# Expert stage: rstd for four tiles at once, scaling eight steps later; the expert weights applied by GpSimd and ScalarE

## The chip, the core and the metric

The kernel runs on one core of a Trainium2 chip. A core has TensorE (matrix products, results in PSUM), VectorE, ScalarE, GpSimd, and SyncE, which here only issues DMAs; each engine runs its own list of instructions in order, and semaphores tie them together. The time is the device time in microseconds (us) of one execution, as the median over several.

## What is computed

Two layers. Layer 0 (attention and feed-forward, eight sequences of 256 tokens, width 128) takes most of the time and isn't touched. The change is in the mixture of experts that ends layer 1, and in the sum that follows it:

```python
logits = xf @ router_w.T + router_b
top_w, top_e = jax.lax.top_k(softmax(logits), 2)          # 16 experts, 2 per token
top_w = top_w / jnp.sum(top_w, axis=-1, keepdims=True)
# for every expert, for the tokens routed to it:
h = jax.nn.silu(xf @ W1.T) * (xf @ W3.T)                  # 128 -> 256
y = h @ W2.T                                              # 256 -> 128
yn = (y - mean(y)) / jnp.sqrt(var(y) + 1e-05) * gm + bt
acc = acc + coeff[:, None] * yn
# and at last, s being layer 1's attention:
x = x + s * silu(acc)
```

## The kernel before

**Stages.** 2048 tokens are 16 tiles of 128 (NT = 16). A loop of four turns computes layer 0 and layer 1's attention; a last section computes routing, and GpSimd scatters every token's row to two places of a scratch tensor in HBM that is sorted by expert (L1854). Then comes the expert stage: CT = 48 tiles of 128 rows, each of one expert. It ends with a gather-free load of the results (they were sent to their tokens' places) and the output.

**The expert stage, tile by tile.** All engines run over steps j = 0 to 47 and a few more, each tile passing down the line:
- ScalarE copies the expert's weights W1, W3, gamma and beta into a ring of places (L1295, 128x768, PLACES = 12, two tiles ahead), applies Silu to the first half of the up product (L1308), and copies turned tokens for each pair of tiles (L1285).
- TensorE turns tokens (L1100), computes the up product (L1112, four 128x128 products a tile) and, two steps later, the down product (L1124, two products). All are recorded at the helper's line L782, the turns at L1100.
- VectorE in step j: statistics of tile j - 3 (bn_stats L1679), scale of tile j - 6 (L1686: YN times rstd plus beta, into the ring YO of eight), aggregate of tile j - 3 (L1692, mean and variance), product of tile j (L1697: Silu times the second half), centring of tile j - 3 (L1701: minus mean, times gamma, into the ring YN of four). SCALE_LAG = 6 is that distance of six.
- GpSimd for each pair of tiles: rstd (the helper at L1779 to L1782: variance plus EPS, then the power -0.5, both on 128x2), after both tiles' aggregates; then a send for each tile, two tiles behind (L1826: an indirect DMA that writes each row of YO to its token's place in HBM). Per pair the order is rstd(t, t+1), send(t-2), send(t-1). The scale of tile t waits for rstd(t, t+1) (c_rstd, L1681), the send of a tile for its scale (c_out), and the scale of tile s for the landing of the send of s - 8 (spread).

**After the last send.** SyncE waits until all sends have landed and loads the results in four groups of four token tiles, each 512 KB (L770, YAB: two results a token). For each group g VectorE multiplies both results by their router weights (L1718, two products of 128x512), adds them (L1722), ScalarE applies Silu (L1313), and VectorE multiplies by S1ALL and adds XALL (L1710, L1711), one group later. SyncE stores each group (L773). Every ScalarE activation is recorded at the helper's line L1132.

Of the kernel before, what the change touches and what calls it, by code (L numbers as in the profile page):

```python
# [18 lines left out]
ALU = mybir.AluOpType  # L19
# [3 lines left out]
P = 128  # L23
D = 128
NB, SEQ = 8, 256
NT = NB * SEQ // P
GT = 4
# [16 lines left out]
class Pair:  # L44
# [8 lines left out]
    def sem(self, n):  # L53
        return self.sems[n % 2]
# [366 lines left out]

DOWN_LAG, CENTRE_LAG, SCALE_LAG = 2, 3, 6

OUT_RING, MULT_RING, TOKEN_RING, NORM_RING = 8, 3, 8, 4

PLACES = 12
WIDE = 2 * FE + 2 * D

T_A0 = T_P_USES // 2
# [6 lines left out]
def gated_layers(nc, ins, out):  # L438
    ctx = ExitStack()
    with ctx:  # L440
# [3 lines left out]
        def sem(name):  # L444
            return ctx.enter_context(nc.semaphore(name))

        def pair(name):
            return Pair(ctx, nc, name)
# [55 lines left out]
        def carve(*shape):  # L504
            n = 1
            for s in shape:
                n *= s
            v = arena[:, at[0]:at[0] + n]
            at[0] += n
            assert at[0] <= ARENA, at[0]  # L510
            if len(shape) == 1:
                return v
            names = "abcd"[:len(shape)]
            return v.rearrange(f"p ({' '.join(names)}) -> p {' '.join(names)}",
                               **{c: s for c, s in zip(names[1:], shape[1:])})
# [105 lines left out]
        WUP = carve(PLACES, WIDE)  # L621
        YN = carve(NORM_RING, D)
        YO = carve(OUT_RING, D)
        YAB = carve(NT, 2, D)
        G2 = carve(2, GT, D)
        G3 = carve(2, GT, D)
# [21 lines left out]
        onehot, gap_done, gap_exp = sem("onehot"), sem("gap_done"), sem("gap_exp")  # L648
        pos_done, q_masked = sem("pos_done"), sem("q_masked")
        pv_done, iota_raw, iotas = pair("pv_done"), sem("iota_raw"), sem("iotas")  # L650
        moe_in, silu_done, out_ready = sem("moe_in"), sem("silu_done"), sem("out_ready")


# [9 lines left out]
        def down_bank(tile):  # L663
            return DOWN_BANKS[tile % len(DOWN_BANKS)][:, 0:D]
# [465 lines left out]
        def _(act):  # L1130
# [149 lines left out]
            def keep_pair(q):  # L1280
                act.wait_ge(c_turned, q + 1)
                t = 2 * q % TOKEN_RING
                if 2 * q >= TOKEN_RING:
                    act.wait_ge(c_up, 2 * q - TOKEN_RING + 2)
                act_fn(XGT[:, t:t + 2, :].rearrange("p j k -> p (j k)"), Tb[0][:, 0:2 * P], ACT.Copy).then_inc(c_ready, 1)  # L1285
# [16 lines left out]
            for j in range(CT):  # L1302
                if j + 2 < CT:
                    place_weights(j + 2)
                act.wait_ge(c_up, j + 1)
                if j >= 2:
                    act.wait_ge(c_mult, j - 1)
                act_fn(HS[:, j % 2, :], up_bank(j)[:, 0:FE], ACT.Silu).then_inc(c_silu, 1)  # L1308
                if j % 2 and j + 3 < CT:
                    keep_pair((j + 3) // 2)  # L1310
            for g in range(NT // GT):
                act.wait_ge(moe_in, g + 1)
                act_fn(G3[:, g % 2].rearrange("p t d -> p (t d)"), G2[:, g % 2].rearrange("p t d -> p (t d)"), ACT.Silu)\  # L1313
                    .then_inc(silu_done, 1)
# [3 lines left out]
        def _(dve):  # L1318
# [9 lines left out]
            def step(instr, carry_wait=True):  # L1328

                steps[1] += 1  # L1330
                instr.then_inc(dstep, 1)
                dve.wait_ge(dstep, steps[0] + steps[1])
                if not carry_wait:
                    settled()
# [337 lines left out]
            for j in range(CT + SCALE_LAG):  # L1672
                tile, scaled = j - CENTRE_LAG, j - SCALE_LAG
                centres = 0 <= tile < CT
                n, w = tile % NORM_RING, WUP[:, tile % PLACES, 2 * FE:WIDE]
                if centres:
                    dve.wait_ge(c_down, tile + 1)
                    settled()
                    V.bn_stats(ST[:, n, 0, :], down_bank(tile)).then_inc(c_bn, 1)  # L1679
                if scaled >= 0:  # L1680
                    dve.wait_ge(c_rstd, scaled // 2 + 1)  # L1681
                    dve.wait_ge(c_centred, scaled + 1)
                    if scaled >= OUT_RING:

                        dve.wait_ge(spread[scaled % OUT_RING], 16 * (scaled // OUT_RING))
                    V.scalar_tensor_tensor(YO[:, scaled % OUT_RING, :], YN[:, scaled % NORM_RING, :],  # L1686
                                           RS[:, scaled % NORM_RING:scaled % NORM_RING + 1],
                                           WUP[:, scaled % PLACES, 2 * FE + D:WIDE], ALU.mult, ALU.add).then_inc(c_out, 1)
                if centres:
                    dve.wait_ge(c_bn, tile + 1)  # L1690
                    settled()
                    V.bn_aggr(MV[:, n, :], ST[:, n, 0, :]).then_inc(c_stats, 1)  # L1692
                if j < CT:
                    dve.wait_ge(c_silu, j + 1)
                    if j >= MULT_RING:
                        dve.wait_ge(c_down, j - MULT_RING + 1)
                    V.tensor_tensor(GTT[:, j % MULT_RING, :], HS[:, j % 2, :], up_bank(j)[:, FE:2 * FE], ALU.mult)\  # L1697
                        .then_inc(c_mult, 1)
                if centres:
                    dve.wait_ge(c_stats, tile + 1)  # L1700
                    V.scalar_tensor_tensor(YN[:, n, :], down_bank(tile), MV[:, n, 0:1], w[:, 0:D], ALU.subtract, ALU.mult)\  # L1701
                        .then_inc(c_centred, 1)
            steps[:] = [c0, 0]

# [7 lines left out]

            for g in range(NT // GT):
                x = slice(g * GT, (g + 1) * GT)
                dve.wait_ge(ld_y[g], 16)
                for k in range(2):
                    y = YAB[:, x, k, :]
                    last = V.tensor_tensor(y, y, WGT[:, k, x].unsqueeze(2).broadcast_to([P, GT, D]), ALU.mult)  # L1718
                step(last)
                if g >= 2:  # L1720
                    dve.wait_ge(silu_done, g - 1)
                V.tensor_tensor(G2[:, g % 2], YAB[:, x, 0, :], YAB[:, x, 1, :], ALU.add).then_inc(moe_in, 1)  # L1722
                if g:
                    output(g - 1)
# [4 lines left out]
        def _(pool):  # L1729
# [49 lines left out]
            def rstd(o, var):  # L1779
                n = var.shape[1]  # L1780
                step(G.tensor_scalar(o, var, EPS, None, ALU.add))  # L1781
                return G.tensor_tensor(o, o, powm[:, 0:n], ALU.pow)  # L1782
# [75 lines left out]

            steps[:] = [step_c0, 0]
            for tile in range(CT):  # L1860
                if tile % 2 == 0:
                    pool.wait_ge(c_stats, tile + 2)
                    if tile >= 4:
                        pool.wait_ge(c_out, tile - 2)
                    rstd(RS[:, tile % 4:tile % 4 + 2], MV[:, tile % 4:tile % 4 + 2, 1]).then_inc(c_rstd, 1)
                if tile >= 2:
                    send(tile - 2)
            send(CT - 2)
            send(CT - 1)


def rope_tables():
# [39 lines left out]
```

## Time and profile before

| | us |
|---|---|
| median of three runs | 936.89 (935.74 to 938.36) |
| profiled execution | 931.56 |
| its span, first to last instruction | 929.7 |

| engine | busy us | share of the span |
|---|---|---|
| TensorE (PE) | 727.6 | 78% |
| VectorE (DVE) | 635.4 | 68% |
| ScalarE (ACT) | 506.0 | 54% |
| GpSimd (POOL) | 391.5 | 42% |

Engines appear in the profile as PE, PEld (TensorE's weight load), DVE, ACT, POOL and SP (SyncE). The table of shares is a mean over stages with different limits. The expert stage starts where the tokens' rows come back from HBM, at about 806 us, and its last send is issued at 907.78; the rest is the final sum. A row of the timeline gives start, duration, engine, line, operation, output and inputs, how often it was repeated, and in square brackets the idle time before it with what ended that. An operation's idle time of kind "issue" is the engine's own sequencing.

### The profile page before, as it was taken

The page shows a single profiled execution, that of the slowest core. Times are in us where ns is not written, and L with a number is a line of the kernel's source. Part 1 is how long each engine was busy: PE and PEld are TensorE (multiplying, and loading weights), DVE is VectorE, ACT ScalarE, POOL GpSimd, SP SyncE. Part 2 cuts the span into 40 slices and gives each one's busy share as a digit, 9 for nine tenths or more (in the row PEclk, how much of TensorE's full clock was granted, in tenths as well). Part 3 has the DMA queues.
Part 4 walks back from the last instruction along what each step waited for, and adds up shares of the span by engine and source line. Part 5 has one row for each costly group of instructions (what it writes and reads, how often), then busy time and mean ns, then how long its engine had stood idle before and what let it go on. Part 6 is the DMA issues. An engine that isn't in the chain of part 4 may idle for free.

```text
span 929.7 us, 19949 instructions
## 1 busy us (share of the span) xinstructions
PE 727.6 (78%) x6997; PEld 547.7 (59%) x7031; DVE 635.4 (68%) x1521; ACT 506.0 (54%) x901; POOL 391.5 (42%) x470
## 2 busy tenths in 40 slices
PE   2589787599898875898988769885997689698840
PEld 1256465367676753576767447762775567598730
DVE  2586685588779664977796759638676499276645
ACT  1255455365766653756766446543656275487711
POOL 4560651670335034705340545009300437458880
PEclk9799998799999997999999979989999599899975
DMA  5700000000000000000000000000000345212104
GB/s 154 213 1 1 1 1 1 1 1 2 1 2 1 2 1 2 1 2 1 2 1 2 1 2 1 2 1 0 2 2 1 92 135 180 84 59 80 59 38 144
DMA packets 41963, 29.70 MB, mean 32 GB/s; under 512 B 7570, under 2 KB 39308, under 8 KB 41612
## 3 DMA queue, kind: packets, MB, share of 16 engines
q1 hardware_dynamic: 39308, 23.18, 8.6%
q0 software_dynamic: 2560, 5.25, 1.5%
q8 instruction: 60, 0.98, 0.4%
q14 instruction: 35, 0.29, 0.1%
HBM read 18.98 MB, written 9.44 MB: 31 GB/s over the span
## 4 chain that ended last, share of the span: by engine, by line
PE 44%; DVE 20%; POOL 12%; issue 12%; ACT 8%; DMA 1%; SPq 1%; DVEq 0%; POOLq 0%; ACTq 0%
PE psM L782 19%; PE psT L821 4%; ACT arena L1132 4%; PE psO L866 4%; PE psS L851 4%; DVE arena L1457 3%; PE psO L782 3%; PE psS L812 3%; DVE PR L1349 3%; POOL arena L1800 3%; POOL arena L1803 3%; POOL yt_scratch L1826 3%; ACT L1132 2%; POOL RS L1782 2%; DVE arena L1465 2%
## 5 line engine op out<-in xcount | busy, mean ns | idle before, releaser
L782 PE MATMUL psM<-arena 128*128 128x128 f32 (+7 forms) x1168 | 269.3, 374 | 48.0 <-DVE arena L1457 30.3
L1132 ACT ACTIVATE arena<-psT 128x512 f32<-128x512 f32 (+3 forms) x296 | 149.6, 530 | 128.6 <-PE psT L821 44.9
L782 PEld LDWEIGHTS psM<-arena 128*128 128x128 f32 (+5 forms) x1168 | 158.6, 193 | 102.0 <-DVE arena L1457 44.3
L1132 ACT ACTIVATE arena<-psM 128x512 f32<-128x512 f32 (+2 forms) x168 | 88.4, 542 | 126.6 <-PE psM L782 125.7
L1781 POOL TENSOR_SCALAR RS<-MV 128x2 f32<-128x2 f32 x56 | 12.9, 231 | 304.0 <-DVE MV L1490 211.6
L1343 DVE TENSOR_REDUCE MX<-psS 128x4 f32<-128x512 f32 (+1 forms) x160 | 102.7, 683 | 44.9 <-PE psS L851 22.9
L1800 POOL TENSOR_TENSOR arena<-arena,powm 128x8 f32<-128x8 f32 x64 | 109.5, 1711 | 5.3
L1132 ACT ACTIVATE PR<-PR 128x512 f32<-128x512 f32 x160 | 94.9, 626 | 21.0 <-DVE PR L1349 20.7
L1349 DVE TENSOR_TENSOR PR<-psS,MX 128x512 f32<-128x512 f32 x160 | 102.2, 680 | 0.0
L821 PE MATMUL psT<-ident,PR 128*128 128x128 f32 x640 | 91.4, 278 | 10.5 <-ACT PR L1132 6.8
L821 PEld LDWEIGHTS psT<-ident,PR 128*128 128x128 f32 x640 | 71.9, 143 | 34.3 <-issue 22.9
L1803 POOL TENSOR_TENSOR arena<-arena 128x512 f32<-128x512 f32 x64 | 84.1, 1313 | 0.0
L1457 DVE TENSOR_TENSOR arena<-psM,arena 128x512 f32<-128x512 f32 x128 | 81.8, 681 | 3.3 <-POOL arena L1803 3.3
L1132 ACT ACTIVATE arena<-arena 128x768 f32 (+3 forms) x61 | 46.5, 763 | 57.1 <-DVE arena L1722 30.2
L1132 ACT ACT_TABLE_LOAD x51 | 65.4, 1283 | 2.1 <-PEq L1904 1.2
L1799 POOL TENSOR_SCALAR arena<-arena 128x8 f32<-128x8 f32 x64 | 18.2, 284 | 109.9 <-DVE arena L1448 109.3
L1465 DVE TENSOR_TENSOR arena<-arena 128x512 f32<-128x512 f32 x64 | 49.9, 802 | 19.8 <-POOL arena L1803 19.8
L782 PEld LDWEIGHTS psO<-arena,PT 128*64 128x64 f32 (+1 forms) x768 | 48.2, 155 | 14.9 <-issue 11.3
L1448 DVE TENSOR_REDUCE arena<-arena 128x8 f32<-128x512 f32 x64 | 43.5, 679 | 19.5 <-ACT arena L1132 19.1
L851 PE MATMUL psS<-arena 32*128 32x256 f32 (+1 forms) x512 | 55.7, 346 | 0.0
L1826 POOL DMA_INDIRECT yt_scratch<-arena,DEST x48 | 49.9, 1040 | 12.2 <-issue 6.7
L782 PE MATMUL psO<-arena,PT 128*64 128x65 f32 (+1 forms) x768 | 51.5, 241 | 2.9 <-ACT PT L1132 2.9
(196 smaller groups left out, 1142.5 us busy)
## 6 DMA issues: line engine op xcount, KB each, us to landing
arena<-in_L_ffn_w SPq DMA_DIRECT2D x50, 128.0 KB, 2.4
xg_scratch<-zeros SPq DMA_DIRECT2D x12, 256.0 KB, 4.0
arena<-xg_scratch SPq DMA_DIRECT2D x12, 256.0 KB
arena<-yt_scratch SPq DMA_DIRECT2D x4, 512.0 KB, 5.3
arena<-in_L_ffn_wqkv SPq DMA_DIRECT2D x2, 768.0 KB, 5.0
arena<-in_L_ffn_ln_g SPq DMA_DIRECT2D x1, 1024.0 KB, 7.5
arena<-in_L_ffn_ln_b SPq DMA_DIRECT2D x1, 1024.0 KB, 10.4
out<-arena SPq DMA_DIRECT2D x4, 256.0 KB, 2.2
```

The costliest lines, as they stand in the source:

```text
L782: return nc.tensor.matmul(o, lhsT, rhs, start=start, stop=stop)
L821: last = nc.tensor.transpose(bank[:, c * P:(c + 1) * P], PR[:, m % 4, c * P:(c + 1) * P], ident[:])
L851: last = nc.tensor.matmul(Sb[i][:, c * keys:(c + 1) * keys], QL[r, b, lane, qt * P:(qt + 1) * P], KT1[r, b * SEQ:b * SEQ + keys], start=False,
L1132: return nc.scalar.activation(o, i, f, **kw)
L1343: V.tensor_reduce(maxima[i], scores[i], AX, ALU.max).then_inc(dstep, 1)
L1349: V.tensor_tensor(PR[:, (n + i) % 4, :].rearrange("p (s k) -> p s k", s=ns), scores[i], maxima[i].unsqueeze(2).broadcast_to([P, ns, 512 // ...
L1448: V.tensor_reduce(SS[:, m % 4, :], SQ[:, m % 2, :].rearrange("p (h d) -> p h d", h=8), AX, ALU.add).then_inc(ss_done.sem(m), 1)
L1457: last = V.tensor_tensor(dst.rearrange("p (h d) -> p h d", h=8), src, RT[:, 2 * l + n % 2, x, t % 2, :].unsqueeze(1) .broadcast_to([P, 8, ...
L1465: V.tensor_tensor(r1, r1, RN[:, m % 4, :].unsqueeze(2).broadcast_to([P, 8, DH]), ALU.mult)\
L1800: G.tensor_tensor(RN[:, m % 4, :], RN[:, m % 4, :], powm[:, 0:8], ALU.pow)
L1803: G.tensor_tensor(r1, r1, r2[:, :, ::-1, :], ALU.add).then_inc(rope_sum.sem(m), 1)
L1826: G.indirect_dma_start(YT, bass.IndirectOffsetOnAxis(DEST[:, tile:tile + 1], 0), YO[:, tile % OUT_RING, :], None)\
```

## The change

- SCALE_LAG goes from 6 to 8, the rings of statistics and of YN (NORM_RING) from 4 to 8, the places for weights from 12 to 14. The expert stage gets its own tiles for statistics, mean and variance, and rstd, in the arena.
- GpSimd computes rstd for four tiles at once (TOGETHER = 4), and sends one tile behind instead of two. Per four tiles the order is rstd(t to t+3), send(t-1), send(t), send(t+1), send(t+2).
- The weighting leaves VectorE. GpSimd multiplies the first result of each group (one product 128x512), after its last send; ScalarE multiplies the second (four Copies 128x128 with a scale per partition), one group ahead of its Silu. VectorE waits for both and adds.

```diff
-DOWN_LAG, CENTRE_LAG, SCALE_LAG = 2, 3, 6
-OUT_RING, MULT_RING, TOKEN_RING, NORM_RING = 8, 3, 8, 4
-PLACES = 12
+DOWN_LAG, CENTRE_LAG, SCALE_LAG = 2, 3, 8
+OUT_RING, MULT_RING, TOKEN_RING, NORM_RING = 8, 3, 8, 8
+PLACES = 14
+TOGETHER = 4
...
+        C_STATS, C_MEAN, C_RSTD = carve(NORM_RING, 6), carve(NORM_RING, 2), carve(NORM_RING)
...
+            def weight_second(g):
+                act.wait_ge(ld_y[g], 16)
+                for t in range(g * GT, (g + 1) * GT):
+                    last = act_fn(YAB[:, t, 1, :], YAB[:, t, 1, :], ACT.Copy, scale=WGT[:, 1, t:t + 1])
+                last.then_inc(second_weighted, 1)
+
+            weight_second(0)
             for g in range(NT // GT):
+                if g + 1 < NT // GT:
+                    weight_second(g + 1)
                 act.wait_ge(moe_in, g + 1)
...
-                    V.bn_stats(ST[:, n, 0, :], down_bank(tile)).then_inc(c_bn, 1)
+                    V.bn_stats(C_STATS[:, n, :], down_bank(tile)).then_inc(c_bn, 1)
                 if scaled >= 0:
-                    dve.wait_ge(c_rstd, scaled // 2 + 1)
+                    dve.wait_ge(c_rstd, scaled // TOGETHER + 1)
...
-                                           RS[:, scaled % NORM_RING:scaled % NORM_RING + 1],
+                                           C_RSTD[:, scaled % NORM_RING:scaled % NORM_RING + 1],
...
-                dve.wait_ge(ld_y[g], 16)
-                for k in range(2):
-                    y = YAB[:, x, k, :]
-                    last = V.tensor_tensor(y, y, WGT[:, k, x].unsqueeze(2).broadcast_to([P, GT, D]), ALU.mult)
-                step(last)
+                dve.wait_ge(first_weighted, g + 1)
+                dve.wait_ge(second_weighted, g + 1)
                 if g >= 2:
                     dve.wait_ge(silu_done, g - 1)
                 V.tensor_tensor(G2[:, g % 2], YAB[:, x, 0, :], YAB[:, x, 1, :], ALU.add).then_inc(moe_in, 1)
...
             for tile in range(CT):
-                if tile % 2 == 0:
-                    pool.wait_ge(c_stats, tile + 2)
-                    if tile >= 4:
-                        pool.wait_ge(c_out, tile - 2)
-                    rstd(RS[:, tile % 4:tile % 4 + 2], MV[:, tile % 4:tile % 4 + 2, 1]).then_inc(c_rstd, 1)
-                if tile >= 2:
-                    send(tile - 2)
-            send(CT - 2)
+                if tile % TOGETHER == 0:
+                    pool.wait_ge(c_stats, tile + TOGETHER)
+                    if tile >= NORM_RING:
+
+                        pool.wait_ge(c_out, tile - NORM_RING + TOGETHER)
+                    x = slice(tile % NORM_RING, tile % NORM_RING + TOGETHER)
+                    rstd(C_RSTD[:, x], C_MEAN[:, x, 1]).then_inc(c_rstd, 1)
+                if tile:
+                    send(tile - 1)
             send(CT - 1)
+            for g in range(NT // GT):
+                x = slice(g * GT, (g + 1) * GT)
+                pool.wait_ge(ld_y[g], 16)
+                G.tensor_tensor(YAB[:, x, 0, :], YAB[:, x, 0, :], WGT[:, 0, x].unsqueeze(2).broadcast_to([P, GT, D]),
+                                ALU.mult).then_inc(first_weighted, 1)
```

## Rows read from the trace of the kernel before

**Rows 1.** Table of stretches: us; busy per engine (instructions); clock; DMA share; GB/s

```profile
838.00:897.00 59.00, 48.60 (x396) 45.24 (x394) 38.17 (x163) 37.41 (x73) 49.17 (x65) 1.00 0.17 59
```

**Rows 2.** Timeline of GpSimd, one pair of tiles in mid stage

```profile
847.64 0.24 POOL L1781 TENSOR_SCALAR RS<-MV 128x2 f32<-128x2 f32 x1
847.96 0.72 POOL L1782 TENSOR_TENSOR RS<-RS,powm 128x2 f32<-128x2 f32 x1
848.88 1.13 POOL L1826 DMA_INDIRECT yt_scratch<-arena,DEST  x1 [0.20 <-issue]
850.31 0.96 POOL L1826 DMA_INDIRECT yt_scratch<-arena,DEST  x1 [0.30 <-DVE arena L1686]
851.30 0.24 POOL L1781 TENSOR_SCALAR RS<-MV 128x2 f32<-128x2 f32 x1
```

**Rows 3.** Timeline, VectorE's two scales of the same pair

```profile
848.72 0.35 DVE L1686 SCALAR_TENSOR_TENSOR arena<-arena,RS 128x128 f32<-128x128 f32 x1 [1.31 <-POOL RS L1782]
...
849.85 0.33 DVE L1686 SCALAR_TENSOR_TENSOR arena<-arena,RS 128x128 f32<-128x128 f32 x1
```

**Rows 4.** Timeline of TensorE, down products of two tiles two apart

```profile
823.06 0.61 PE L782 MATMUL psT<-arena 128*128 x4
...
825.96 0.61 PE L782 MATMUL psO<-arena 128*128 x4
```

**Rows 5.** Groups by line and shape: count, busy us, mean ns, idle before: the power

```profile
L1800 POOL TENSOR_TENSOR arena<-arena,powm 128x8 f32<-128x8 f32 x64 | 109.5, 1711 | 5.3
...
L1782 POOL TENSOR_TENSOR RS<-RS,powm 128x2 f32<-128x2 f32 x56 | 40.5, 723 | 4.7
```

**Rows 6.** Timeline of GpSimd: second rstd, first and last send

```profile
821.90 0.23 POOL L1781 TENSOR_SCALAR RS<-MV 128x2 f32<-128x2 f32 x1 [1.65 <-DVE MV L1692]
...
823.11 1.07 POOL L1826 DMA_INDIRECT yt_scratch<-arena,DEST  x1 [0.18 <-issue]
...
907.78 0.96 POOL L1826 DMA_INDIRECT yt_scratch<-arena,DEST  x1 [0.30 <-issue]
```

**Rows 7.** Timeline of VectorE: the scales in steps 8, 9 and 10

```profile
824.39 0.33 DVE L1686 SCALAR_TENSOR_TENSOR arena<-arena,RS 128x128 f32<-128x128 f32 x1
...
825.85 0.33 DVE L1686 SCALAR_TENSOR_TENSOR arena<-arena,RS 128x128 f32<-128x128 f32 x1
...
827.33 0.34 DVE L1686 SCALAR_TENSOR_TENSOR arena<-arena,RS 128x128 f32<-128x128 f32 x1
```

**Rows 8.** Timeline of VectorE after the last send: its first and its last operation

```profile
913.88 1.29 DVE L1718 TENSOR_TENSOR arena<-arena,WGT 128x512 f32<-128x512 f32 x2 [9.61 <-DMA arena<-yt_scratch]
...
926.31 0.69 DVE L1711 TENSOR_TENSOR arena<-arena,XALL 128x512 f32<-128x512 f32 x1
```

**Rows 9.** Timeline in layer 0, both engines reading SBUF: VectorE from 208.09, GpSimd

```profile
208.09 2.37 DVE L1465 TENSOR_TENSOR arena<-arena 128x512 f32<-128x512 f32 x2
...
208.30 1.61 POOL L1803 TENSOR_TENSOR arena<-arena 128x512 f32<-128x512 f32 x1
```

**Rows 10.** Timeline in the routing: a GpSimd send and VectorE's operation beside it

```profile
777.98 1.89 POOL L1854 DMA_INDIRECT xg_scratch<-XN1ALL,POSU  x1 [0.30 <-issue]
...
777.82 1.22 DVE L1659 TENSOR_TENSOR arena<-arena 128x1024 bf16<-128x1024 f32 x1
```

**Rows 11.** View of single lines: count, ns min/median/max, first and last start, shape

```profile
L1803 POOL TENSOR_TENSOR arena<-arena x64: 1253/1272/1702, 23.6 to 653.7; 128x512 f32<-128x512 f32 x64
...
L1814 POOL TENSOR_SCALAR arena<-arena,lanem x32: 917/922/1032, 190.6 to 745.2; 128x256 f32<-128x256 f32 x32
```

**Rows 12.** Groups by shape, ScalarE, without and with scale and bias per partition

```profile
L1132 ACT ACTIVATE arena<-psM 128x256 f32<-128x256 f32 x40 | 14.2, 375 | 34.6 <-PE psM L782 34.6
L1132 ACT ACTIVATE arena<-psT,arena 128x256 f32<-128x256 f32 x16 | 9.0, 561 | 18.2 <-PE psT L985 18.2
```

**Rows 13.** View of the results' scratch tensor: its four loads

```profile
L770 SPq DMA_DIRECT2D arena<-yt_scratch x4: 359/934/1447, 910.1 to 912.4; - x4
...
DMA to landing us min/median/max: 3.8/5.3/5.9
```

More of the change, by code:

```diff
@@ L650, in gated_layers @@
         pv_done, iota_raw, iotas = pair("pv_done"), sem("iota_raw"), sem("iotas")
+        first_weighted, second_weighted = sem("first_weighted"), sem("second_weighted")
         moe_in, silu_done, out_ready = sem("moe_in"), sem("silu_done"), sem("out_ready")
@@ L1691, in _ @@
                     settled()
-                    V.bn_aggr(MV[:, n, :], ST[:, n, 0, :]).then_inc(c_stats, 1)
+                    V.bn_aggr(C_MEAN[:, n, :], C_STATS[:, n, :]).then_inc(c_stats, 1)
                 if j < CT:
@@ L1700, in _ @@
                     dve.wait_ge(c_stats, tile + 1)
-                    V.scalar_tensor_tensor(YN[:, n, :], down_bank(tile), MV[:, n, 0:1], w[:, 0:D], ALU.subtract, ALU.mult)\
+                    V.scalar_tensor_tensor(YN[:, n, :], down_bank(tile), C_MEAN[:, n, 0:1], w[:, 0:D], ALU.subtract, ALU.mult)\
                         .then_inc(c_centred, 1)
```

## The prediction

> **What bounds the kernel now.** I read the table of stretches first, because the change touches only the expert stage and what follows it. In the middle of that stage, 838 to 897 us, no compute engine is full: TensorE 48.6 of 59 us, VectorE 38.2, ScalarE 37.4, GpSimd 49.2 [rows 1]. But the profile counts an issuing interval of GpSimd as idle, so its timeline has to be read next. One pair of tiles there is add EPS 0.24, a gap of 0.08, power 0.72, 0.20 of issue, a send of 1.13, 0.30 of issue, a send of 0.96, and 0.03 later the next add: 3.66 us, with no place in it where GpSimd waits for anybody [rows 2]. VectorE's timeline says the same from the other side: in each pair its first scale (L1686) has stood idle for 1.31 us, released by GpSimd's power, and the second scale starts 1.13 after the first [rows 3]. Without that wait VectorE needs 3.66 - 1.31 = 2.35 us a pair. TensorE, while it was the limit, needed 2.90 (823.06 to 825.96) [rows 4]. So the expert stage runs at GpSimd's 3.66, and a faster GpSimd gains until 2.90. TensorE's granted clock is 1.00, its 2.4 GHz level, through this stretch [rows 1] and stays out of the sum. After the last send (907.78) the kernel is a chain: send landed, load of the gathered results, then VectorE back to back from 913.88 to 927.0, then the last store [rows 6, 8].
>
> **Deviations of four tiles at once.** Twelve groups of four replace 24 pairs. The only unknown is the power on 128x4. On 128x2 it takes 723 ns, on 128x8 1711 [rows 5]; a straight line gives 1.05; the mean of the wide ones holds some that were disturbed, so I take 1.04. Bounds: 0.72 (width free below four) and 1.44 (twice the pair). The add, 0.24 now, I take at 0.25 [rows 2]. A cycle of four tiles becomes: send 1.13, three times (0.30 + 0.96), 0.03, add 0.25, 0.08, power 1.04, 0.20 of issue = 6.51 us, against 2 x 3.66 = 7.32. TensorE's floor for four tiles is 5.80, so GpSimd stays the bound, by 0.70.
>
> **Scaling eight steps later.** The first deviation now needs four tiles of statistics. They are there at 821.8 (the second pair's add starts at 821.90 [rows 6]), so the wide one ends about 823.3. The send of tile 0 no longer follows the scale of step 6 but that of step 8, which started at 824.39 [rows 7]: with its 0.33 and some 0.3 of waking and issue it starts at 825.0, not 823.11 [rows 6]. Sends of tiles 1 and 2 follow the scales of steps 9 and 10 (825.85, 827.33 [rows 7]), so at 826.5 and 827.97; the second wide deviation runs 829.0 to 830.34, and the send of tile 3 starts at 830.54. From there GpSimd is continuous: ten cycles of 6.51 to the send of tile 43 (895.64), 1.43 and three times 1.26 to that of tile 47: 900.85. Before it was 907.78 [rows 6]. The stage gives **6.9 us**. (Had the late start cost nothing, 11 cycles would have given 8.9.)
>
> Does the new wait hold GpSimd? The deviation of four needs the statistics of step t+6, the scale reads it in step t+8. When it ends, VectorE, which waits in step t+8, is released; GpSimd issues four sends, 5.1 us, before it wants the statistics of step t+10. VectorE needs under three steps for that, 3 x 1.13 from its own work (4.4 at TensorE's pace). Slack 0.7 or more. Sends sit one tile closer to their scales than before; each needs the scale of a tile whose step is 1.13 after the last, against 1.26 between sends, so none waits. ScalarE's copies of weights wait for the scale of a tile further back; with the places raised from 12 to 14 that distance is as it was. The eight-deep ring YO: the scale of tile s needs the send of s-8 landed, issued 5 us or more before. All at nothing; if the first slack were gone, every us past it costs 11 us in all.
>
> **A port between VectorE and GpSimd.** The trace shows the two holding each other up. At 208.09 two VectorE adds with both inputs in SBUF take 2.37 together (two such operations undisturbed: 1.29 [rows 8]), around a GpSimd add that itself takes 1.61 instead of some 1.27 [rows 9]: GpSimd waited for the running add, and then the next VectorE add waited for the whole of GpSimd's. A send is held too: 1.89 instead of 0.96, under a VectorE tensor_tensor of 1.22 begun just before [rows 10]. So the 1.13 of the first send after a deviation is 0.96 plus what is left of the scale (it runs from 848.72 to 849.07, the send starts at 848.88 [rows 2, 3]). I keep that 0.17 once in four tiles; the other three start some 0.1 to 0.3 after a scale has ended.
> The Trainium skill (SBUF — State Buffer, Who interferes with whom) infers that a tensor_tensor leaves descriptor generation alone, since that needs only the write interface. By it no send would ever pay for a scale: the sum would stay as it is, and rival (d) and half of (b) below would fall away. Rows 10 say otherwise for these indirect sends, and I go by the rows.
>
> **Weighting moved off VectorE.** Removed: eight VectorE products, 1.29 for two [rows 8], some 1.23 with the overlap of 0.07 into the next; 4 x 1.23 = 4.9 us of a chain that is solid VectorE. Added: GpSimd, four products 128x512; the add of that size has 1.27 as its median, 1.25 as its least [rows 11], and I take 1.26, since it too reads two tensors. The bound above is the product with a scalar per partition, 0.92 for half the size, so 1.8 [rows 11]; ScalarE, 16 Copies of 128x128 with a scale per partition. Its rows: 128x256 from PSUM is 0.38, with a scale and a bias per partition 0.56 [rows 12], so 0.09 for one; 128x128 then some 0.4, overlapping by 0.1, four of them 1.3. The loads of y land 3.8 to 5.9 us after issue, the first at 913.88, the last near 918.3, 1.5 apart [rows 13].
> Without the port: first sum can start at 915.37 (913.95 + 1.26, ScalarE 1.3), the second after its landing, 916.8; ScalarE does the second group's weighting before its first Silu, so output 0 starts 917.6; then VectorE is solid: 4 outputs of 1.3 and 2 sums of 0.65, end 924.1. That would be 2.9 less than 927.0.
> With the port: every remaining VectorE operation reads two SBUF tensors, and so does GpSimd's. Sum 0 runs 915.37 to 916.05 and holds product 1 back to 917.3. GpSimd's product 2 follows at once, sum 1 waits behind it to 918.53 and ends 919.2, holding product 3, which gets in before output 0 and runs to 920.4. Left are then four outputs of 1.25 and two sums of 0.63: 926.7. Gain **0.3 us**. (With products of 1.8, the same steps end at 928.9, 1.9 later than now.) The forecast takes this case, as rows 9 show just this alternation with these two kinds of operation.
> The same page of the Trainium skill states it as a rule: a VectorE instruction with two SBUF inputs and a GpSimd instruction that reads SBUF exclude each other for the whole instruction. By that rule the tail gives 0.3, by no rule 2.9; the trace agrees with the rule.
>
> **Sum.** Profiled execution 931.56 (span 929.7): minus 6.9, minus 0.3, 924.4. The median of the three runs is 936.89; the profiled one lies 5.3 under it, and I assume the gap is the same for both kernels: 936.89 - 7.2 = **929.7**.
>
> **Rivals.** (a) *The tail is free of the port*: stage 6.9, tail 2.9, 927.1. For it: product 3 and the two Silus may interleave more kindly than I drew. Against it: rows 9. With the narrow power as well (0.72, 11 x 0.32 = 3.5) it is 923.6.
> (b) *Power grows with width, or sends meet scales*: at 1.44 the cycle is 6.91, 11 x 0.40 = 4.4 is lost, which makes 934.1. The same happens if each of the other three sends pays 0.17: 0.51 x 11 = 5.6, 935.3. For it: VectorE is released in bursts, and later steps of a burst may be set by TensorE. Against: the line between two widths, and the distances above.
> (c) *The late start eats what the cycle gives, no change*: a cycle of 7.1 or more, 936 to 939. It needs both halves of (b), or one with products of 1.8.
> (d) *Slower*: the sends fall into step with the scales. VectorE's scale of 0.34 reads two SBUF tensors; if in the cycle each of three sends starts with a scale just begun, each pays 0.34, the cycle is 6.51 + 1.02 = 7.53, and 11 x 1.02 = 11.2 is lost: 929.7 + 11.2 = 940.9. It decides against the change from 0.22 us a send (7.2 / 33). Against it: the second send of each pair does not pay now [rows 2].
> (e) *The change doesn't do what it says*: the power is issued for four tiles, but VectorE, not GpSimd, turns out to set the pace. VectorE's 2 x 2.35 = 4.7 per four tiles excludes it.
>
> **How the numbers follow.** The forecast with its small variations 0.60; (a) 0.14; (b) 0.17; (c) 0.05; (d) 0.04. I leave (c), (d) and the far end of (a) outside, reach to 925.3 (half of the narrow power with the free tail) and to 934.4 (inside b). About 0.3% (2.8 us) is what a measurement of this kernel tells from no change, so faster ends at 934.1: the forecast, (a) and about two thirds of (b), 0.86; same 0.09, slower 0.05.
>
> **What would show each step.** Timeline of GpSimd in mid stage: a power on 128x4 of 1.04 and 6.51 us from one to the next; first send near 825.0 and last near 900.9; the scale still waits for the power, about 1.8 us once in four tiles (6.51 less 4.7). If instead GpSimd idles before the add, the new wait binds and the forecast is wrong. If sends two to four of a cycle read more than 0.96, it is (b) or (d). In the tail: GpSimd products of 1.7 and VectorE sums of 1.8 mean the port; 1.27 and 0.69 mean (a); 1.8 for the very first product, which nothing disturbs, means the dear product.

## The result and the profile after

| | before | changed |
|---|---|---|
| median of 14 runs each, us | 934.45 | 928.75 |
| span of the profiled execution, us | 929.7 | 924.1 |

The ratio is 0.9937, with a 95% interval from 0.9918 to 0.9956: 0.63% or about 5.9 us faster (the medians differ by 5.7), where 7.2 were forecast against the first three runs.

To see where the time went I cut both profiled executions at the same events: VectorE's first product in the expert stage, the last send, the first operation on loaded results, VectorE's last end, and the end of the span.

| stretch, us | before | changed | difference | forecast |
|---|---|---|---|---|
| start to first product (nothing changed here) | 814.53 | 815.37 | +0.84 | 0 |
| first product to last send | 93.25 | 87.01 | -6.24 | -6.9 |
| last send to first operation on its results | 6.10 | 6.33 | +0.23 | 0 |
| from there to VectorE's last end | 13.12 | 12.65 | -0.47 | -0.3 |
| to the end of the span | 2.70 | 2.74 | +0.04 | 0 |

The first line is scatter, not the change: over all kernels shown below, whose work up to there is the same, it lies between 813.4 and 818.3. The spans of single profiles should therefore be compared by stretches.

The timeline of GpSimd in the changed kernel, mid stage, one cycle of four tiles; it answers to [rows 2]:

```profile
849.74 0.25 POOL L1791 TENSOR_SCALAR arena<-arena 128x4 f32<-128x4 f32 x1
850.08 1.04 POOL L1792 TENSOR_TENSOR arena<-arena,powm 128x4 f32<-128x4 f32 x1
851.32 1.15 POOL L1836 DMA_INDIRECT yt_scratch<-arena,DEST  x1 [0.20 <-issue]
852.77 0.96 POOL L1836 DMA_INDIRECT yt_scratch<-arena,DEST  x1 [0.30 <-DVE arena L1699]
854.04 0.96 POOL L1836 DMA_INDIRECT yt_scratch<-arena,DEST  x1 [0.30 <-DVE arena L1699]
855.30 0.96 POOL L1836 DMA_INDIRECT yt_scratch<-arena,DEST  x1 [0.30 <-issue]
856.28 0.25 POOL L1791 TENSOR_SCALAR arena<-arena 128x4 f32<-128x4 f32 x1
```

From add to add it is 6.54 us, still without a wait: the gap ahead of a send is the 0.30 of issue whatever the profile names as its releaser, and ahead of the add it is 0.02. The power on 128x4 takes 1.04. From the same timeline the first and the last send, which answer to [rows 6], and between them VectorE's scale that waits for the power, which answers to [rows 3]:

```profile
826.11 1.09 POOL L1836 DMA_INDIRECT yt_scratch<-arena,DEST  x1 [1.66 <-DVE arena L1699]
...
851.15 0.35 DVE L1699 SCALAR_TENSOR_TENSOR arena<-arena 128x128 f32<-128x128 f32 x1 [1.91 <-POOL arena L1792]
...
902.38 0.96 POOL L1836 DMA_INDIRECT yt_scratch<-arena,DEST  x1 [0.30 <-issue]
```

The end of the kernel, which answers to [rows 8]: the timeline of all engines from the first loaded group on.

```profile
908.71 1.28 ACT L1136 ACTIVATE arena<-arena,WGT 128x128 f32<-128x128 f32 x4 [21.55 <-DMA arena<-yt_scratch]
908.76 1.03 POOL L1884 TENSOR_TENSOR arena<-arena,WGT 128x512 f32<-128x512 f32 x1 [5.42 <-DMA arena<-yt_scratch]
910.09 0.69 DVE L1732 TENSOR_TENSOR arena<-arena 128x512 f32<-128x512 f32 x1 [11.99 <-ACT arena L1136]
...
912.37 1.12 POOL L1884 TENSOR_TENSOR arena<-arena,WGT 128x512 f32<-128x512 f32 x1 [0.69 <-DMA arena<-yt_scratch]
912.50 1.53 DVE L1723 TENSOR_TENSOR arena<-arena,S1ALL 128x512 f32<-128x512 f32 x1
...
914.07 0.69 DVE L1724 TENSOR_TENSOR arena<-arena,XALL 128x512 f32<-128x512 f32 x1
914.10 1.55 POOL L1884 TENSOR_TENSOR arena<-arena,WGT 128x512 f32<-128x512 f32 x1 [0.62 <-DMA arena<-yt_scratch]
914.68 1.53 DVE L1732 TENSOR_TENSOR arena<-arena 128x512 f32<-128x512 f32 x1
...
919.95 0.69 DVE L1723 TENSOR_TENSOR arena<-arena,S1ALL 128x512 f32<-128x512 f32 x1 [0.48 <-DMA out<-arena]
```

Here is the port. VectorE's output at 912.50 stands behind GpSimd's product that began at 912.37 and ends at 913.49: 1.53 instead of 0.68. GpSimd's last product begins at 914.10 under a running VectorE operation and takes 1.55 instead of 1.03; the sum at 914.68 then waits for it, 1.53 again. These are the only two operations of VectorE in the tail that the port stretches. Two things in these rows were not in the forecast: the groups land 1.8 us apart, and the last output (919.95) waits 0.48 for a store to leave its buffer.

### The profile page after: what moved, and what is told of

Same layout as the page of the kernel before. It is cut to its first block, busy times and chain, and to the rows that moved or that the text cites. A ratio compares the mean times of both kernels' runs of the same rounds, so it can differ in the third digit from the quotient of the medians.

```text
span 924.1 us, 19925 instructions
## 1 busy us (share of the span) xinstructions
PE 724.8 (78%) x6997; PEld 546.0 (59%) x7031; DVE 632.7 (68%) x1513; ACT 510.2 (55%) x917; POOL 387.6 (42%) x450
## 4 chain that ended last, share of the span: by engine, by line
PE 45%; DVE 19%; issue 12%; POOL 12%; ACT 8%; DMA 2%; SPq 1%; DVEq 0%; ACTq 0%; POOLq 0%
PE psM L786 19%; PE psT L825 5%; ACT arena L1136 5%; PE psO L870 4%; PE psS L855 4%; DVE arena L1470 3%; PE psO L786 3%; PE psS L816 3%; POOL yt_scratch L1836 3%; DVE PR L1362 3%; POOL arena L1813 3%; POOL arena L1810 3%; ACT L1136 2%; DVE arena L1461 1%; DVE arena L1478 1%
## 5 line engine op out<-in xcount | busy, mean ns | idle before, releaser
L1791 POOL TENSOR_SCALAR RS<-MV 128x2 f32<-128x2 f32 x32 | 7.2, 224 | 286.4 <-DVE MV L1503 211.8
```

## The experiments

e3, e4, e5, e6, e10 and e11 were executed once each; of these only the stretches and rows of their profiles are used.

**Which half of the change gives the gain.** Stage alone (VectorE weights as before), and tail alone (the stage as before):

```diff
-                dve.wait_ge(first_weighted, g + 1)
-                dve.wait_ge(second_weighted, g + 1)
+                dve.wait_ge(ld_y[g], 16)
+                for k in range(2):
+                    y = YAB[:, x, k, :]
+                    last = V.tensor_tensor(y, y, WGT[:, k, x].unsqueeze(2).broadcast_to([P, GT, D]), ALU.mult)
+                step(last)
```

That is e1_stage_alone against the changed kernel (weight_second and GpSimd's products go too). e2_tail_alone is the kernel before with the same lines the other way round, and with weight_second and the products added.

> Only the expert stage is changed (deviations of four, scales eight steps later); VectorE weights both results as before. Read as two stretches: from VectorE's first product to the last send (before 93.25 us, after 87.01), and from the first VectorE operation after the last send to VectorE's last end (before 13.12). Theory, the stage carries nearly all: 87.0 and 13.1, ratio to the kernel before about 0.994. Rival, the moved weighting carries a good part of the gain: then this kernel stands at 0.996 or above.

> Only the weighting is moved; the stage is as before. Theory, the port between VectorE and GpSimd gives back most of what is taken off VectorE: stage 93.3, from the landing of the first results to VectorE's last end 12.7 instead of 13.1, ratio 0.9995, no measurable difference. Rival, the port costs little: 10.5 and a ratio of 0.997.

| | first product to last send | to first operation | to VectorE's last end | ratio to before (95%) |
|---|---|---|---|---|
| before | 93.25 | 6.10 | 13.12 | |
| changed | 87.01 | 6.33 | 12.65 | 0.9937 (0.9918 to 0.9956) |
| e1_stage_alone | 86.38 | 6.40 | 13.12 | 0.9945 (0.9918 to 0.9972) |
| e2_tail_alone | 92.74 | 6.12 | 12.24 | 0.9997 (0.9978 to 1.0017) |

The stage carries the gain: its stretch is as short in e1 as in the changed kernel, and without it (e2) nothing is left in the runs. The interval of e1 alone would allow the 0.996 of the rival too. The moved weighting by itself can't be told from no change, though its stretch is 0.9 us shorter in the profile. It is 12.24 there and 12.65 in the changed kernel, with the same instructions; that is followed up below. The stage's 0.6 of difference between two kernels with the same stage is how far the start of the stage scatters (first send 10.03 after the first product in one, 10.74 in the other).

**What the later scale costs.** The changed kernel with deviations of two tiles:

```diff
-TOGETHER = 4
+TOGETHER = 2
```

> The changed kernel with deviations of two tiles again, everything else kept: scales eight steps later, rings of eight. The later scale alone. Theory: the first send comes 10.6 after the first product (before 8.6), GpSimd has one pair's deviation more behind it, 23 cycles of 3.66 follow as before: from the first product to the last send 96.0, 2.8 more than in the kernel before. Rival: the later scale costs nothing, 93.3.

First send 10.76 after the first product, last send 96.36: 3.1 us later than before. The first send accounts for 2.2 of it; the other 0.9 is about one pair's deviation, which stood ahead of the first send and now stands behind it, as e5 also keeps the new order of the sends. The whole run took 938.32 beside 930.31 for the kernel before on the same chip, but those are one run each, and the kernel before alone ranges over 9 us. Moving the scale is a pure cost, and the groups of four pay for it.

**What GpSimd's adds and powers hide.** The changed kernel without them:

```diff
-                    dve.wait_ge(c_rstd, scaled // TOGETHER + 1)
+                    dve.wait_ge(c_stats, scaled + 1)
...
-                                           C_RSTD[:, scaled % NORM_RING:scaled % NORM_RING + 1],
+                                           C_MEAN[:, scaled % NORM_RING, 1:2],
...
-                if tile % TOGETHER == 0:
-                    pool.wait_ge(c_stats, tile + TOGETHER)
...
-                    rstd(C_RSTD[:, x], C_MEAN[:, x, 1]).then_inc(c_rstd, 1)
                 if tile:
                     send(tile - 1)
```

> The changed kernel without any add and power on GpSimd in the expert stage: VectorE scales by the variance itself, the deviation is left out. GpSimd has only sends, 1.26 a tile. Theory, TensorE is the next bound at 2.90 a pair: from the first product to the last send 74 to 76 us instead of 87.0. Rival, VectorE or ScalarE sets 1.6 a tile: 80. Of the sends: if the 1.13 of a cycle's first send is a wait for the scale running beside it, sends above 0.96 stay wherever a scale has begun just before; if it is the price of the first send after another GpSimd operation, none is left but the first.

77.42 us instead of 87.01, a little over the 74 to 76, with the first send at 11.45 after the first product instead of 10.7 (why it is later wasn't followed up). The table of stretches of this kernel (columns as in [rows 1]):

```profile
838.00:885.00 47.00, 46.90 (x421) 46.71 (x419) 40.31 (x165) 38.65 (x79) 30.91 (x33) 1.00 0.25 82
```

Its timeline, two sends a pair apart and two of TensorE's down products a pair apart:

```profile
854.34 0.95 POOL L1836 DMA_INDIRECT yt_scratch<-arena,DEST  x1 [0.39 <-DVE arena L1699]
...
855.30 0.61 PE L786 MATMUL psO<-arena 128*128 x4
...
857.24 0.95 POOL L1836 DMA_INDIRECT yt_scratch<-arena,DEST  x1 [0.36 <-DVE arena L1699]
...
858.19 0.61 PE L786 MATMUL psO<-arena 128*128 x4
```

TensorE is busy 46.90 of 47 us and both engines step by 2.9 us a pair: the floor that the prediction took from [rows 4]. GpSimd now waits for VectorE ahead of sends. On the sends' own price this run says half: without powers none of the 48 reads over 0.96, but none of them starts inside the stretch of a scale that costs (below), so it doesn't speak of the port.

**Where the 1.13 of a cycle's first send comes from.** The prediction gave it to the port. First a memset, then a power, ahead of the fourth send of a cycle:

```diff
+                if tile % TOGETHER == 3:
+                    G.memset(POOL_SPARE[:], 0.0)
                 if tile:
                     send(tile - 1)
```

In e11_power_before_send the new line is `G.tensor_tensor(POOL_SPARE[:], WGT[:, 0, 0:2], powm[:, 0:2], ALU.pow)`.

> The changed kernel with a GpSimd memset of 128x2 before the fourth send of every cycle of four. If the first send's 1.13 is a wait for VectorE's scale, the fourth send stays at 0.96 and the cycle grows by the memset alone. If a send costs more after any other GpSimd operation, the fourth send reads about 1.13 too and the cycle grows by that besides.

> The changed kernel with one more power of 128x2 (its result isn't used) ahead of the fourth send of each cycle of four; a memset there left that send at 0.96. If the send after a power costs more by itself, the fourth reads about 1.07 though no scale runs beside it; if the 1.15 of the first send is all a wait for the scale, the fourth stays at 0.96. The cycle grows from 6.55 to about 7.2 either way, as in the rival (a price of the power by its count), and the last send comes 7 us later.

The timeline of e6, a second send with VectorE's scale beside it, and a fourth send behind its memset:

```profile
833.35 0.33 DVE L1700 SCALAR_TENSOR_TENSOR arena<-arena 128x128 f32<-128x128 f32 x1
...
833.44 1.09 POOL L1837 DMA_INDIRECT yt_scratch<-arena,DEST  x1 [0.30 <-issue]
...
848.89 0.12 POOL L1880 MEMSET POOL_SPARE<- 128x2 f32 x1
849.20 0.97 POOL L1837 DMA_INDIRECT yt_scratch<-arena,DEST  x1 [0.19 <-issue]
```

The timeline of e11, a fourth send behind its power, with VectorE's last scale before it and the next one after it:

```profile
848.14 0.33 DVE L1700 SCALAR_TENSOR_TENSOR arena<-arena 128x128 f32<-128x128 f32 x1
...
848.60 0.73 POOL L1880 TENSOR_TENSOR POOL_SPARE<-WGT,powm 128x2 f32<-128x2 f32 x1
849.52 1.03 POOL L1837 DMA_INDIRECT yt_scratch<-arena,DEST  x1 [0.19 <-issue]
...
852.00 0.35 DVE L1700 SCALAR_TENSOR_TENSOR arena<-arena 128x128 f32<-128x128 f32 x1 [2.63 <-POOL arena L1793]
```

A send after a memset costs what the others cost, and the memset's 0.12 fits into the gap of issue (the cycle stays 6.54 to 6.57). A send after a power costs 1.03 though the scale at 848.14 had ended a microsecond before: 0.07 go with the power. And a second send, with no power ahead of it, reads 1.09 where a scale had begun 0.09 before it (833.44): the port is real too, as in [rows 10]. The power itself shows its price: the cycle grows from 6.55 to 7.27 and the last send comes at 95.44, 8.4 us later, where 7 were expected.

How the 1.15 splits is read from other sends. The changed kernel's very first send (826.11, shown further up) stands behind a power of 128x4. Its timeline, the scale before that send, and a second send of a cycle with the scale before it:

```profile
825.48 0.34 DVE L1699 SCALAR_TENSOR_TENSOR arena<-arena 128x128 f32<-128x128 f32 x1
...
832.93 0.33 DVE L1699 SCALAR_TENSOR_TENSOR arena<-arena 128x128 f32<-128x128 f32 x1
...
833.06 1.03 POOL L1836 DMA_INDIRECT yt_scratch<-arena,DEST  x1 [0.30 <-issue]
```

The same of e4, its very first send, with no power ahead of it:

```profile
828.75 0.96 POOL L1836 DMA_INDIRECT yt_scratch<-arena,DEST  x1 [22.27 <-DVE arena L1699]
```

The first send, at 826.11, starts 0.29 after its scale has ended and still reads 1.09; without powers it reads 0.96. So 0.13 goes with the power of 128x4, although that had ended 1.66 us earlier. The send at 833.06 meets the last 0.20 of a scale and reads 0.07 more than 0.96; the first send of a cycle meets the last 0.18. The 1.15 is therefore nearer to 0.96 + 0.13 + 0.06, and the scale has the smaller part. Why the power of 128x2 in e11 left only 0.07 is open. In all kernels here, sends behind another send read 1.01 to 1.09 where a scale had begun 0.09 to 0.17 before them (12 sends), and 0.95 to 0.97 where it had begun 0.19 or more before; sends that started within 0.02 of a scale's start read 0.96.

**What the port costs in the tail.** Without GpSimd's products, and with them only for the groups where VectorE is idle anyway:

```diff
-                V.tensor_tensor(G2[:, g % 2], YAB[:, x, 0, :], YAB[:, x, 1, :], ALU.add).then_inc(moe_in, 1)
+                if g < 2:
+                    V.tensor_tensor(G2[:, g % 2], YAB[:, x, 0, :], YAB[:, x, 1, :], ALU.add).then_inc(moe_in, 1)
+                else:
+                    for t in range(g * GT, (g + 1) * GT):
+                        last = V.scalar_tensor_tensor(G2[:, g % 2, t % GT, :], YAB[:, t, 0, :], WGT[:, 0, t:t + 1],
+                                                      YAB[:, t, 1, :], ALU.mult, ALU.add)
+                    last.then_inc(moe_in, 1)
```

That is e7_products_two_groups, whose GpSimd loops over two groups and whose VectorE waits for it in those two only. In e3_no_gpsimd_product the loop on GpSimd and VectorE's wait for it are gone, and the sum is as in the changed kernel.

> The changed kernel without GpSimd's four products: the first result of each token goes into the sum unweighted, that part of the computation is left out. ScalarE's part, the loads and VectorE's work are the same. Theory, the port: VectorE's sums and outputs all at 0.69, and from the first landing to VectorE's last end 10.2 instead of 12.65. Rival, the loads that land 1.8 apart and ScalarE's weighting ahead of its Silu set the tail: 12 or more.

> The changed kernel, with GpSimd's product only for groups 0 and 1, where VectorE has idle time anyway; for groups 2 and 3 VectorE multiplies and adds in one pass (four scalar_tensor_tensor of 128x128 a group, some 1.15 us, instead of a sum of 0.69). If the port is what makes the tail long, from the first landing to VectorE's last end it is 11.1 instead of 12.65 (after), although VectorE has more work; if VectorE's work or the loads set it, 13.0 or more.

The stretch from the first landing to VectorE's last end is 12.65 in the changed kernel, 10.90 without the products, 11.36 with two of them. So the products beside VectorE cost 1.75 us, and the two stretched operations, 1.53 instead of 0.68 and 0.69, are 1.69 of it: that is the port. Giving VectorE more work (1.13 for a multiply and add of four tiles, against 0.69 for the sum) makes the tail 1.3 us shorter, since nothing then stands in its way (11.1 were expected for the 11.36; the intervals of the whole runs of e7 and of the changed kernel overlap, so this too rests on the profile). The 10.90 is over the 10.2 expected: 0.49 of it is the wait for a store's buffer, and the second group lands 1.8 after the first. VectorE's timeline without the products:

```profile
910.30 0.69 DVE L1731 TENSOR_TENSOR arena<-arena 128x512 f32<-128x512 f32 x1 [11.92 <-ACT arena L1136]
912.10 0.69 DVE L1731 TENSOR_TENSOR arena<-arena 128x512 f32<-128x512 f32 x1 [1.11 <-ACT arena L1136]
912.71 0.68 DVE L1723 TENSOR_TENSOR arena<-arena,S1ALL 128x512 f32<-128x512 f32 x1
...
918.47 0.69 DVE L1723 TENSOR_TENSOR arena<-arena,S1ALL 128x512 f32<-128x512 f32 x1 [0.49 <-DMA out<-arena]
```

**Why the loads land later.** In the kernel before and in e2_tail_alone the four loads move about 347 GB/s and land up to 5.9 us after issue [rows 13]; in the changed kernel and in every other one up to here it is about 290 GB/s and up to 7.0 or 7.1. e1_stage_alone has the tail of before and is slow, e2_tail_alone has the new tail and is fast, so it isn't what the engines do meanwhile; what goes with it is the layout. The new tiles for statistics (48 + 16 + 8 numbers) push YAB from a multiple of 512 bytes in the arena to 288 past one. (The arena itself starts at byte 65024 of a partition, 127 times 512; in e6 and e11 POOL_SPARE moves it 32 bytes on, which puts YAB at 320 past a multiple.)

```diff
+        carve(56)
         YAB = carve(NT, 2, D)
```

That is e9_results_at_512; e10_results_at_64 has 8 in place of 56.

> The changed kernel with 56 unused numbers (224 bytes) a partition ahead of the tile for the results (YAB). The change put 72 new numbers there, so YAB begins 288 bytes past a multiple of 512 (before: at a multiple of 512, counted in the arena), and in every run with the new layout its loads move 290 GB/s instead of 347. Theory, the start address: with the padding the loads are back at 347 GB/s and land 3.8 to 5.9 after issue instead of 4.0 to 7.0; from the last send to the first operation 6.1 instead of 6.33, from there to VectorE's last end 12.2 instead of 12.65: 0.6 to 0.7 us in all. Rival, what slows the loads is ScalarE and GpSimd working beside them, or chance: 290 GB/s as now.

> As e9_results_at_512 with only 8 numbers (32 bytes) of padding: YAB begins at 320 past a multiple of 512, at a multiple of 64. If it is a boundary of 64 bytes that matters, the loads move 347 GB/s; if one of 512, they stay at 290 or between.

Two microseconds in the middle of the loads, from the table of stretches (the last column is GB/s), first in the kernel before:

```profile
914.40:916.40 2.00, 0.00 (x0) 0.00 (x0) 1.97 (x4) 0.47 (x1) 0.00 (x0) 0.50 1.15 347
```

The same in the changed kernel, and from the view of its load line the landings, which answer to [rows 13]:

```profile
909.20:911.20 2.00, 0.00 (x0) 0.00 (x0) 0.69 (x1) 1.47 (x6) 1.23 (x2) 0.50 1.16 291
```

```profile
DMA to landing us min/median/max: 4.0/6.0/7.0
```

In e9:

```profile
908.10:910.10 2.00, 0.00 (x0) 0.00 (x0) 0.69 (x1) 1.78 (x7) 1.54 (x2) 0.50 1.15 347
```

```profile
DMA to landing us min/median/max: 3.8/5.4/5.9
```

In e10:

```profile
907.40:909.40 2.00, 0.00 (x0) 0.00 (x0) 0.69 (x1) 1.46 (x6) 1.23 (x2) 0.50 1.17 290
```

```profile
DMA to landing us min/median/max: 4.1/6.1/7.0
```

With YAB back at a multiple of 512 the loads are at 347 GB/s, beside the same work of ScalarE and GpSimd. From the last send to the first operation it is 6.16, the tail 12.23: 0.6 us less in all, as expected. At 320 past a multiple of 512, which is a multiple of 64, nothing changes. The whole kernel came to 0.9918 (0.9888 to 0.9947) of before; its interval overlaps that of the changed kernel, so the 0.6 us rests on the profile.

The Trainium skill (DMA: Bandwidth & Descriptors, How a descriptor splits into AXI transactions) says that a transaction of at most 256 bytes starts at a multiple of 256, so that a descriptor that doesn't start at one also pays for the bytes before it. Each packet here is 512 bytes; by that account (an estimate) it takes three transactions instead of two at both 288 and 320, and both are slow, so the runs agree with the page in that. The page also counts beats of 32 bytes, by which such packets would cost 6% and 12% more (an estimate), while both measure the same, 290 for 347 GB/s. Nor do the runs show 256 itself: none put YAB at an odd multiple of it, and the page's account is of a descriptor's reads, while here the misplaced end is the one written.

**Putting the findings together.** e7 with the first four tiles in two pairs and their scales six steps later (e8), and that with the padding of e9 as well (e12). GpSimd's loop follows GROUPS too; that part isn't shown:

```diff
 TOGETHER = 4
+GROUPS = [(0, 2), (2, 2)] + [(t, 4) for t in range(4, CT, 4)]
+STEP_OF = {s: s + (6 if s < 4 else 8) for s in range(CT)}
...
-                tile, scaled = j - CENTRE_LAG, j - SCALE_LAG
+                tile = j - CENTRE_LAG
+                scaled = next((s for s in STEP_OF if STEP_OF[s] == j), -1)
```

> As e7_products_two_groups, and the first four tiles go in two pairs with scales six steps later; from tile 4 on groups of four and eight steps. If the late start costs what the prediction put on it, the first send comes 8.6 us after the first product instead of 10.7, the cycle stays 6.55, and the last send comes 1.5 us earlier than in the changed kernel: 85.5 instead of 87.0. Rival: the ring and TensorE's pace take it up later, 87.0. Ratio to the kernel before 0.991 against 0.9925.

> The early start, GpSimd's product for groups 0 and 1 only, and the padding, together. From the first product to the last send 85.4, to the first operation after it 6.1, from there 10.9: against the changed kernel 1.6 + 0.2 + 1.7 = 3.5 us less, 9.4 less than the kernel before, ratio 0.990. If the parts overlap, 2 us less than the changed kernel and 0.992.

| | first send | last send | to first operation | to VectorE's last end | median, us | ratio to before (95%) |
|---|---|---|---|---|---|---|
| changed | 10.74 | 87.01 | 6.33 | 12.65 | 928.75 | 0.9937 (0.9918 to 0.9956) |
| e7_products_two_groups | 10.74 | 87.00 | 6.39 | 11.36 | 925.62 | 0.9919 (0.9888 to 0.9950) |
| e8_early_start | 7.07 | 85.44 | 6.41 | 11.35 | 925.92 | 0.9918 (0.9887 to 0.9948) |
| e12_best | 7.06 | 85.52 | 6.07 | 11.23 | 923.96 | 0.9900 (0.9874 to 0.9925) |

(The two sends are counted from the first product.) The early start gives its 1.5 us in the stretch, though between e7 and e8 the runs show no difference. Its first send came at 7.07 where 8.6 were expected, because it now stands ahead of the second pair's deviation; of these 3.7 us against the changed kernel 1.6 are left at the last send, as GpSimd then waits for VectorE, 0.93 us ahead of its third add and 0.37 and 0.71 ahead of two sends. So the rival of e8, that the pace of the others takes it up, is right for the larger half. From GpSimd's timeline of e8:

```profile
829.92 0.23 POOL L1801 TENSOR_SCALAR arena<-arena 128x4 f32<-128x4 f32 x1 [0.93 <-DVE arena L1708]
...
834.60 0.96 POOL L1846 DMA_INDIRECT yt_scratch<-arena,DEST  x1 [0.71 <-DVE arena L1702]
```

e12 is 3.2 us below the changed kernel over the three stretches, 1.49 + 0.26 + 1.42, where 3.5 were expected (its tail is 11.23 and not 10.9), and 1% below the kernel before. Its interval overlaps the end of that of the changed kernel, so as a whole the step from one to the other is likely and not settled.

## Why the prediction came out right, point by point

- **The bound.** GpSimd sets the stage's pace, by its own instructions and their issue, though the table shows it idle for a sixth of the time [rows 1, 2]. Right: removing instructions from it shortened the cycle by what they cost, adding one in e11 lengthened it by what it cost, and removing all deviations uncovered TensorE's 2.90 a pair. Adding up the timeline with the gaps between instructions was what showed it.
- **The power on 128x4.** The line between two widths [rows 5] gave 1.05, taken as 1.04, and 1.04 was measured. The cycle is 6.54 against 6.51 forecast; over ten cycles and one second send at 1.03 that makes 0.4 of the missing 0.7.
- **The late start.** Forecast 10.5 from the first product to the first send (825.0 less 814.53), measured 10.74; that is most of the rest. The prediction put the late start at 2.0 (8.9 less 6.9). No run measures it by itself in this kernel; e5 (3.1 us with pairs, 2.2 of it from the first send) and e8 (1.5 us back) lie on either side.
- **The new wait.** It never held GpSimd; VectorE waits 1.91 once in four tiles where 1.8 was forecast.
- **The first send of a cycle.** The step that called the 1.13 "0.96 plus what is left of the scale" was wrong in its cause: some 0.13 is the price of a send that follows the power and only 0.06 is the scale's. The number came out right (1.15 for 1.13) because both stay once a cycle, and that is luck: a change that took away only the scale or only the power would have been misjudged. Rival (d), sends falling into step with scales, happened for single sends (1.03 in the changed kernel, 1.09 in e6) and never for a whole stage.
- **The tail.** The port did what [rows 9] show, with 1.53 and 1.55 where "1.8" and "1.7" were named as its marks, but it held VectorE twice and not at every meeting. The gain of 0.47 against 0.3 came out near by luck, from errors that cancel. GpSimd's product is cheaper than the add it was priced by [rows 11], 1.03 instead of 1.26. And the loads are slower, which no step foresaw: the prediction took the landings 1.5 us apart from [rows 13] and didn't ask where the new tiles push YAB. That edit was costed at nothing and cost 0.6 us. With the loads at their old pace, the moved weighting gives 0.9 (13.12 less 12.23), with the port still in it. The wait for a store's buffer, 0.48 here, was in no term either; the kernel before has none.
- **Sum.** In the profile 5.6 us, after a loss of 0.84 to the scatter of the part before the stage; 6.4 us come from the parts that changed, where 7.2 were forecast. The interval of the runs, 4.1 to 7.7 us, holds both. The median of 928.75 lies nearer to the forecast 929.7 than the gain does to 7.2, and that is luck: the three first runs of the kernel before lay 2.4 us over its median of fourteen.

## What to carry to other kernels

Where one engine's instruction stream is the bound, add its durations and its issue gaps from the timeline: the busy share alone hides the bound, and each instruction less is worth its full length until the next engine's period. Work moved off VectorE to GpSimd loses part of its worth where VectorE reads two SBUF tensors at that time; here a fused multiply and add on VectorE beat the same work on GpSimd (11.36 us for 12.65). And a new small tile in a hand-carved memory moves all that stands behind it: check where the destinations of large loads come to lie; multiples of 512 bytes were fast here.

## What the runs showed of the hardware

- Loads of 512 KB in packets of 512 bytes ran at 347 GB/s into a tile that starts at a multiple of 512 bytes in the arena, and at 290 GB/s into one that starts 288 or 320 past one.
- An indirect send by GpSimd took 0.96 us, 1.03 behind the added power of 128x2 in e11, 1.09 behind one of 128x4 with no scale beside it, 0.96 to 0.97 behind a memset. Behind another send it took 1.01 to 1.09 only where VectorE's scale had begun 0.09 to 0.17 before. A memset of 0.12 between two sends cost nothing: the gap of issue shrank from 0.30 to 0.19.
- GpSimd's product of 128x512 with a weight broadcast along the row took 1.03 us undisturbed, the add of two full tensors of that size 1.27.
